# Reading the spare bank ahead of the maxima, and spreading the ungrouping copies, in four attention stages of a sixteen-stage kernel

## The reference

```python
scores = jnp.einsum('bhqd,bhkd->bhqk', q, k) / jnp.sqrt(jnp.float32(D_K))
scores = jnp.where(causal, scores, -jnp.inf)
attn = _my_softmax(scores, axis=-1)          # exp(x - max) / (sum + eps)
ctx = jnp.einsum('bhqk,bhkd->bhqd', attn, v)
...
return ctx @ Wo.T + bo
```

## Time and profile before

| | |
|---|---|
| median of 3 runs | 4516.43 us (4515.83 to 4519.06) |
| profiled execution | 4499.53 us, span 4497.8 us |
| granted TensorE clock, mean | 0.804 |
| TensorE busy | 3027.0 us, 67% |
| VectorE busy | 2776.0 us, 62% |
| GpSimd busy | 2034.3 us, 45% |
| ScalarE busy | 1710.5 us, 38% |
| ungrouping copies (L1007), 128 | 39.6 us in all, mean 310 ns |
| l0b, steps with exponentials | 582 to 1105 us |
| l2a | 2214 to 2568 us |
| l2b | 2856 to 3212 us |
| l3a | 3494 to 3848 us |

### The profile page before, as it was taken

How to read it: one execution, slowest core, us unless ns; L and a number is a source line. 1 busy time by engine, 2 the same in 40 slices (tenths; PEclk the granted TensorE clock), 3 DMA queues, 4 the chain that set the end, 5 groups by cost and what they waited for, 6 DMA issues and landing times. The chain is left out here.

```text
span 4497.8 us, 67760 instructions
## 1 busy us (share of the span) xinstructions
PE 3027.0 (67%) x23775; PEld 1875.0 (42%) x23775; DVE 2776.0 (62%) x5980; ACT 1710.5 (38%) x3042; POOL 2034.3 (45%) x2610
## 2 busy tenths in 40 slices
PE   5858277776286568659587756777566888466856
PEld 3658112121286248558233334333243344244534
DVE  4634477774534852342577578677487767495778
ACT  2413256665122223434355512455422455223511
POOL 6553320100243313232445376354595454595776
PEclk9879578887588669879699867799777999586967
DMA  5122222210122012002221000222001211000000
GB/s 157 39 71 76 66 82 66 63 53 1 49 90 61 9 44 70 19 25 63 73 79 66 23 1 1 86 72 73 2 0 44 72 66 52 1 1 1 1 1 19
DMA packets 217167, 206.35 MB, mean 46 GB/s; under 512 B 49431, under 2 KB 194007, under 8 KB 216072
## 3 DMA queue, kind: packets, MB, share of 16 engines
q1 hardware_dynamic: 204552, 176.85, 12.2%
q0 software_dynamic: 12288, 25.19, 1.8%
HBM read 103.55 MB, written 96.47 MB: 44 GB/s over the span
## 5 line engine op out<-in xcount | busy, mean ns | idle before, releaser
L942 DVE TENSOR_REDUCE l0b_negm<-l0b_ps_s 128x2 f32<-128x1024 f32 x256 | 304.2, 1220 | 139.0 <-PE l0b_ps_s L713 138.3
L802 ACT ACTIVATE l0b_E<-l0b_ps_t 128x1024 f32<-128x1024 f32 x256 | 262.0, 1023 | 198.3 <-PE l0b_ps_t L695 197.9
L942 DVE TENSOR_REDUCE l2b_negm<-l2b_ps_s 128x2 f32<-128x256 f32 (+3 forms) x256 | 199.2, 819 | 83.2 <-PE l2b_ps_s L719 82.9
L942 DVE TENSOR_REDUCE l3a_negm<-l3a_ps_s 128x2 f32<-128x256 f32 (+3 forms) x256 | 199.1, 818 | 79.7 <-PE l3a_ps_s L719 79.2
L942 DVE TENSOR_REDUCE l2a_negm<-l2a_ps_s 128x2 f32<-128x256 f32 (+3 forms) x256 | 198.6, 819 | 73.7 <-PE l2a_ps_s L719 73.4
L802 ACT ACTIVATE l3a_E<-l3a_ps_t 128x768 f32<-128x768 f32 (+1 forms) x192 | 169.2, 881 | 166.7 <-PE l3a_ps_t L695 166.4
L802 ACT ACTIVATE l2a_E<-l2a_ps_t 128x768 f32<-128x768 f32 (+1 forms) x192 | 169.4, 882 | 162.6 <-PE l2a_ps_t L695 162.4
L802 ACT ACTIVATE l2b_E<-l2b_ps_t 128x768 f32<-128x768 f32 (+1 forms) x192 | 169.4, 882 | 143.0 <-PE l2b_ps_t L695 142.9
L883 POOL TENSOR_SCALAR_AFFINE_SELECT l2b_E<-l2b_E 128x256 f32<-128x256 f32 x256 | 101.0, 408 | 214.0 <-ACT l2b_E L802 213.8
L883 POOL TENSOR_SCALAR_AFFINE_SELECT l3a_E<-l3a_E 128x256 f32<-128x256 f32 x256 | 101.0, 407 | 200.2 <-ACT l3a_E L802 198.2
L883 POOL TENSOR_SCALAR_AFFINE_SELECT l2a_E<-l2a_E 128x256 f32<-128x256 f32 x256 | 101.0, 407 | 198.3 <-ACT l2a_E L802 196.0
(11 more groups left out here) (1013 smaller groups left out, 9392.2 us busy)
## 6 DMA issues: line engine op xcount, KB each, us to landing
room_up<-l0b_stack SPq DMA_DIRECT2D x32, 192.0 KB
room_down<-l0b_stack SPq DMA_DIRECT2D x32, 192.0 KB
room_up<-l2a_stack SPq DMA_DIRECT2D x32, 192.0 KB
room_down<-l2a_stack SPq DMA_DIRECT2D x32, 192.0 KB
room_up<-l2b_stack SPq DMA_DIRECT2D x32, 192.0 KB
room_down<-l2b_stack SPq DMA_DIRECT2D x32, 192.0 KB
room_up<-l3a_stack SPq DMA_DIRECT2D x32, 192.0 KB
room_down<-l3a_stack SPq DMA_DIRECT2D x32, 192.0 KB
```

The lines of the kernel that those rows point to most:

```text
L802: act.activation(probs(n % 3, c, 0)[:, 2 * p:2 * p + 2, :], ps_t[:, :, 0:width[c]], ACT.Exp, scale=scale).then_inc(probs_ready.sem, 1)
L942: e = dve.tensor_reduce(negm[:, qt, :, j], ps_s[n % 2][:, :, off:off + keys[qt]], AX.X, ALU.max, negate=True)
```

## The change

In VectorE's loop, `weighted` (l = 4) and `add_output` (group 1, l = 2) move ahead of `maxima` in their step, in all four stages. In l0b alone the 16 ungrouping copies are laid one a step on the steps of `UNGROUP_AT`, 5 to 24 of the next batch, and `ao` gets a second tile, so that sums of the next batch don't overwrite what is still to be copied; the copies of the last batch for which no step is left follow the loop. The total of instructions is the same.

```diff
@@ -447,7 +447,7 @@
 K_ROWS = (slice(2, 5), slice(0, 6, 5), slice(1, 2))
 STACK = 48
 M_ROW = 48
-UNGROUP = (0, 3, 6, 7, 10, 13, 16)
+UNGROUP_AT = (5, 6, 8, 9, 10, 11, 13, 14, 15, 16, 17, 18, 19, 21, 22, 24)
 
 
 def heads_attention_stage(core, name, w, wo=None, bo=None, qk_bias=None, v_bias=None, rope=None, eps=0.0,
@@ -495,7 +495,7 @@
         oT = sb("oT", [P, S])
         den = sb("den", [P, TB, 4])
         rec = sb("rec", [P, TB, 4])
-        ao = sb("ao", [P, TB, D])
+        ao = [sb(f"ao{u}", [P, TB, D]) for u in range(2 if grouped else 1)]
         if projected:
             aoT = sb("aoT", [P, S])
         y = sb("y", [P, TB, D])
@@ -767,7 +767,7 @@
                         mm = pe.transpose(ps_x[:, t * P:(t + 1) * P], oT[:, t * P:(t + 1) * P], core.identf[:, :])
                 elif what == "attnT":
                     for t in range(TB):
-                        mm = pe.transpose(ps_x[:, t * P:(t + 1) * P], ao[:, t, :], core.identf[:, :])
+                        mm = pe.transpose(ps_x[:, t * P:(t + 1) * P], ao[0][:, t, :], core.identf[:, :])
                 else:
                     for t in range(TB):
                         mm = pe.matmul(ps_x[:, t * P:(t + 1) * P], aoT[:, t * P:(t + 1) * P], wo[:, :], start=True, stop=True)
@@ -991,21 +991,20 @@
                 c = G % QUADS * 32
                 if projected and c == 0 and G > 0:
                     in_spare(dve, "attnT", G // QUADS - 1)
-                dve.tensor_tensor(ao[:, :, c:c + 32].rearrange("p t (h d) -> p t h d", d=HD),
+                dve.tensor_tensor(ao[G // QUADS % len(ao)][:, :, c:c + 32].rearrange("p t (h d) -> p t h d", d=HD),
                                   pv[:, :, :, 0:HD], r, ALU.mult).then_inc(spare_read.sem, 1)
 
-            def ungroup(n, part):
-
-                if part == 0:
+            def ungroup(n, k):
+
+                i, j = k // 4, k % 4
+                if k == 0:
                     dve.wait_ge(spare_read.sem, spare_read.upto(use["back", QUADS * n + 3] + 1))
                     if n >= 1:
                         dve.wait_ge(out_read.sem, out_read.upto(n))
-                for k in range(UNGROUP[part], UNGROUP[part + 1]):
-                    i, j = k // 4, k % 4
-                    src = ao[:, :, :].rearrange("p k (t i d) -> p t k i d", t=4, i=4)[32 * j:32 * j + 32, :, :, i, :]
-                    dst = y[:, :, :].rearrange("p t (k j d) -> p t k j d", k=4, j=4)[32 * i:32 * i + 32, :, :, j, :]
-                    e = dve.tensor_copy(dst, src)
-                if part == len(UNGROUP) - 2:
+                src = ao[n % 2][:, :, :].rearrange("p k (t i d) -> p t k i d", t=4, i=4)[32 * j:32 * j + 32, :, :, i, :]
+                dst = y[:, :, :].rearrange("p t (k j d) -> p t k j d", k=4, j=4)[32 * i:32 * i + 32, :, :, j, :]
+                e = dve.tensor_copy(dst, src)
+                if k == len(UNGROUP_AT) - 1:
                     e.then_inc(out_ready.sem, 1)
 
             def add_output(n):
@@ -1039,10 +1038,12 @@
             rows.statistics(dve, ch, 1)
             rows.shifts(dve, 1)
             for T, b, g, l in steps():
+                if l == 4 and 0 <= QUADS * b + g - 1 < QUADS * B:
+                    weighted(QUADS * b + g - 1)
+                if g == 1 and l == 2 and projected and 0 <= b - 1 < B:
+                    add_output(b - 1)
                 if 0 <= T + 3 * L < ALL:
                     maxima(T + 3 * L)
-                if l == 4 and 0 <= QUADS * b + g - 1 < QUADS * B:
-                    weighted(QUADS * b + g - 1)
                 if g == 0 and 0 <= b + 2 < B:
                     if rope is not None and l in (0, 1, 2, 5):
                         rotate({0: "q", 1: "q_swapped", 2: "k", 5: "k_swapped"}[l], b + 2)
@@ -1055,12 +1056,10 @@
                     rows.shifts(dve, n)
                 for n in named(counted, T):
                     rows.statistics(dve, ch, n)
-                if grouped and 0 <= b - 1 < B and 0 <= g * L + l - 5 < len(UNGROUP) - 1:
-                    ungroup(b - 1, g * L + l - 5)
+                if grouped and 0 <= b - 1 < B and g * L + l in UNGROUP_AT:
+                    ungroup(b - 1, UNGROUP_AT.index(g * L + l))
                 if g == 0 and l == L - 1 and 0 <= b < B:
                     split_maxima(2 * b + 1)
-                if g == 1 and l == 2 and projected and 0 <= b - 1 < B:
-                    add_output(b - 1)
                 if g == 1 and l == 5 and v_bias is not None and 0 <= b + 1 < B:
                     n = b + 1
                     in_spare(dve, "v", n)
@@ -1073,6 +1072,10 @@
                     split_maxima(2 * (b + 1))
                 if g == 3 and l == 0 and out_normed and 0 <= b - 1 < B:
                     normalise(b - 1)
+            if grouped:
+                for k, at in enumerate(UNGROUP_AT):
+                    if at >= L + 3:
+                        ungroup(B - 1, k)
             if out_normed:
                 normalise(B - 1)
             dve_step.per = ch.k
```

## The result

The changed kernel takes 4395.8 us (median of 4 runs, 4391.5 to 4403.0); the kernel before took 4516.1 us beside it (4508.9 to 4519.1). The ratio of the runs is 0.9737, 95% interval 0.972 to 0.9755: 119 us or 2.6% less by the ratio, 120 us by the medians, against a forecast of 90 us and 4426.4 us. It lies inside the range of 4392 to 4472, 4 us from its lower end.

A forecast was written before the change was run, and what follows sets the result against it. No engine is full; a circle of waits paces the four stages, TensorE often waiting for VectorE. Causal stages 65.5 (73.5 less 8) plus l0b 24.5 make 90 us off: 4426.4 us, range 4392 to 4472.

The forecast's parts named there:

- signs of being right: `ao` and `y` waits under 5 us; l2a, l2b, l3a 19 to 25 shorter each, l0b 20 to 30; copy mean under 0.31.
- `v`: Causal stages, value projection (L757): its waits for `ao` all go once `back` is read in VectorE's idle time, 26.2 us.
- Output product: Causal stages, transposes of the maxima after the output product (L762): waits for `y` all go, 26.3 us.
- Swapped keys: l2a and l3a, swapped key projection (L753): of 13.2 us waiting for `ao`, 10 times 0.7 = 7 us.
- Maxima: Causal stages, score products' waits for `negm`: 14 of 30.4 us (6, 4 and 4), bounds 0 and 30.
- The 8 us taken off: Causal stages: TensorE, coming sooner, meets ScalarE still copying `oT`; about 0.3 us in 21 places, with odd ends 8 us.
- the term for the clock: l0b: shorter waits keep the clock nearer 2.4 GHz; 5 us at half clock in five batches, 3 us, bounds 0 and 12.
- The collisions: l0b steps 8 to 11: single copies meeting GpSimd; one collision, 1 us, bounds 0 and 4 x 1.2 us a batch.
- More comes back: Rival: causal `negm` waits but 5 go (11 us more), 10 more in l0b, 9 of clock: 120 us, 4396; chance 0.09.
- half of the 90: Rival: waits move on to VectorE's rotations, `oT` or the DMA of the maxima; only half gained, 4471; chance 0.13.
- the DMA of the maxima: Next thing late after the causal edits: placing the maxima; covered by 0.75 us, else each 0.1 us short costs 2 us.
- first reduction of a score pair: Rival, slower: it becomes the gate since reads precede it; 105 us added against 90 - 14 won, 4545; chance 0.03.

The follow-up runs named there:

- first fillers: Kernel before plus five needless products per l0b batch (from the second) in TensorE's wait at step 10, three ahead of the first score pair, two ahead of the second: 4499.0 us.
- copies spread: Kernel before with only the ungrouping copies laid one a step and the second tile for the sums; maxima stay first: 4471.4 us, ratio 0.9946.
- late copies: Changed kernel with the 16 ungrouping copies on steps 11 to 30, none on steps 5 to 10: 4365.6 us, ratio 0.9726.
- one copy: Changed kernel with one plain 128 x 512 copy per batch on step 24 in place of the 16 ungrouping copies: 4364.5 us, ratio 0.9719.
- reads first: Kernel before with only `weighted` and `add_output` moved ahead of the maxima in all four stages, ungrouping copies as before: 4394.6 us, ratio 0.9776.
- `weighted` only: Kernel before with only `weighted` (l = 4) moved ahead of the maxima; `add_output` stays behind them: 4424.8 us, ratio 0.9855.
- second profile: The changed kernel run once more, nothing altered: 4391.8 us, ratio 0.9728.
- fillers: Needless products in TensorE's step-10 wait: five on the kernel before, 4499.0 us; three on the reads-moved kernel, 4403.5; two on the changed kernel with needless VectorE reductions, 4400.0.
- the stop: Changed kernel with two needless VectorE reductions of 128 x 1024 ahead of `split_maxima` in batches 1 to 7 of l0b: 4397.6 us, ratio 0.9795.

## Why the prediction was right, and where its sizes were not

**The mechanism.** TensorE's waits for the spare bank were on the path: moving `weighted` and `add_output` alone gives 101 us of the 119 (first experiment), and leaving `add_output` out gives 30 of them back. Of the signs of being right, the waits for `ao` and `y` came out at 4.3 us (under 5 forecast), l0b's copies at a mean of 0.27 us and its waits for `negm` at 15.5 (about 17); the stages gained as forecast or more. The sizes were too small by a third, and the time is in the range with some luck: its lower end was made of a larger gain for `negm` and of at most 12 us for the clock, and the gain for `negm` was no larger.

**Causal stages, 65.5 forecast, 82.5 measured.** By terms, in l2a, l2b and l3a: `v` 26.2 forecast, the waits for `ao` are gone. Output product 26.3 forecast; 1.5 left. Swapped keys 7 forecast of 13.2: here I was too careful, since the wait for `ao` went whole and only 2.1 us for `k_turn` at L770 came in its place. Maxima 14 forecast; 30.4 fell to 17.9, so 12.5, of which l2b gave 2.9 of my 4. The 8 us taken off: the waits for `oT` grew by 3.7, 1.5 and 2.5 us, 7.7 in all, which was right; but in l2b 3.3 us of waits for `m_piece` and in all three 6.9 us for `mT` went too, which the sum did not have. It did not have the growth of others either: 7.9 us for ScalarE's exponentials and 3.0 for GpSimd's masking. With these, all of TensorE's waits in the three stages fell by 66.6 us, 1.1 us from the forecast, its misses having cancelled. The rest is TensorE's busy time, 16.6 us less, 13.6 of it in l3a, whose clock was 0.94 before and 0.98 after in the two profiles. Against the run with 0.98 and the old order (348.1 us) l3a gained 23.2 and the three stages 73.1.

**l0b, 24.5 forecast, 43.5 measured.** The step that failed is the term for the clock, "I take 3, bounds 0 and 12", together with how the waits were added. The waits for `negm` came out as forecast: 31.1 to 15.5 (17 forecast). But `ao` left 2.8 of 8.8, by the collision at step 11, and the waits for ScalarE's exponentials grew by 10.5 and those for `mT` by 3.9, so that TensorE's waits as a whole fell only from 127 to 121 us. What fell is its busy time, 388.3 to 351.5 us with the same instructions. In the third batch, from the transposed scores of step 8 to those of step 16, the kernel before takes 23.16 us and the changed one 17.50. Of these 5.66 us, all waits of TensorE together make 2.1 (8.07 to 6.00; those for `negm` alone 5.23 to 1.79); the remaining 3.6 are instructions that took half again to twice as long in the old one: 1.94 us in place of 1.06 for the value products, 1.86 for 1.16 in the projection. In 737 to 742 us the clock is 1.00 where the earlier trace rows have 0.50.

**What the lower clock cost.** The granted clock in these traces is 1.00 or 0.50 and nothing between, so its time at 0.50 can be added up for a stage. Stages of the same code in different profiles then give a price:

| stage, code (profiles) | length, us | at 0.50, us |
|---|---|---|
| l2a, old order (before, first fillers, copies spread) | 354.1, 356.6, 361.6 | 19.5, 28.7, 47.4 |
| l3a, old order (copies spread, before) | 348.1, 357.5 | 13.4, 44.1 |
| l2a, new order (late copies, one copy, changed) | 325.0, 327.0, 329.0 | 14.2, 20.5, 28.5 |
| l0b, reads first (`weighted` only, both) | 499.1, 506.1 | 116.8, 144.3 |
| l0b, changed (first profile, second) | 479.9, 479.9 | 87.3, 104.5 |

From the ends of the first three rows, a microsecond at the lower clock makes a causal stage 0.27 to 0.31 us longer. In l0b the two rows give 0.25 and 0, but the batches of equal programs, compared one by one (three pairs of profiles, 24 pairs of batches), give 0.27 by a line through zero. The changed kernel spends 87 us of l0b at 0.50 (105 in the second profile), where the kernel before spends 179; so, as an estimate, 20 to 25 of the 43.5 us go with the clock, and 19 to 24 are left for the waits, where the forecast had 21.5 without its clock term. The first two experiments agree: reads first, 34 us less at 0.50, so 9 of the 17.3 us, and 8 left for the 8.8 of `ao`; copies spread, 65 us less, so 18 of the 31.3, and 13.6 left for the 14 forecast. The term was mis-sized because it took one stretch of 5 us in five batches, 25 us; the kernel before has 84 us at 0.50 in steps 10 to 15 alone, of which 5 are left (24 in the second profile), and 69 in steps 16 to 23, of which 55 are left.

That is a rate between profiles, not an experiment on the clock. Where only the clock was treated, nothing was won: fillers left l0b at 523.3, 516.5 and 497.9 us against 523.4, 506.1 and 485.5. The first fillers did cut the time at 0.50 by 51 us, worth 14 at this rate, and the added products cost as much. What they also show is that slow TensorE and late VectorE lie side by side: with either left, the other's gain is met by a wait (1.59 us at 740.82). The changed kernel shortened VectorE's queue, and then both went. A treatment of the clock that adds no work was not found.

**The collisions, 1 us a batch forecast.** In the third batch three of the four single copies on steps 8 to 11 met GpSimd's split, against the one that I counted, and cost 1.7 us more than undisturbed copies (0.60 + 1.14 + 0.63 - 3 x 0.22); over the five batches with splits it is 1.2 us a batch. But my picture of the group was wrong as well: the 2.59 us in the earlier trace rows are three copies and not one, and all three were drawn out (line L1007 of the kernel before in 738 to 741 us: duration in ns, min/median/max, as in the earlier trace rows):

```profile
L1007 DVE COPY l0b_y<-l0b_ao x3: 661/678/1223, 738.1 to 739.4; 32x128 f32<-32x128 f32 x3
```

In the whole stage the kernel before has 22 copies over 0.3 us and the changed one 14, and the copies' time fell from 39.6 to 34.0 us: spreading them made fewer collisions, not more. Moving them behind the split left 5 and won 9.9 us in l0b. The Trainium skill (SBUF — State Buffer, Who interferes with whom) tells of such a meeting as a lock on a port pair, and the drawn-out copies agree. The reductions of l0b kept 1.21 to 1.23 us, beside the same GpSimd instructions too. The same section of the Trainium skill says that this reduction never contends on this chip; the trace agrees.

**The rivals.** The time is that of "More comes back" (120 us, 4396), which I gave 0.09, and so is l0b's sum: 24.5 + 10 + 9 = 43.5. That is luck on its side too, for its terms are only half right: `negm` gave nothing beyond my own forecast, 17.9 us of it and not 5 stayed in the causal stages, and what came instead were `mT`, the swapped keys and TensorE's faster instructions. The others fell: `oT` took 7.7 us and not half of the 90, the DMA of the maxima appears in no list, and no first reduction of a score pair became a gate.

## What to carry to other kernels

When an engine has a read that frees a bank and a reduction whose input the same producer issues later, put the read first: it fits into the idle time, and the length of the producer's wait in the timeline is nearly what it is worth. Small copies of VectorE belong where it idles and where GpSimd is quiet, not just apart from each other; leaving them out altogether (a run with one plain copy) says in one number whether a place is free. Compare stage by stage over several profiles, and look at the time at the lower clock beside the length: two stages of equal code differed by up to 9 us with it, and a gain below that is told apart only between profiles with the same share of slow time.

## What I had not expected of the hardware

- Time outside the edited stages came in two levels, 2902 to 2908 and 2918 to 2926 us, as it seems by set of runs.
- The same stage with the same program varied with TensorE's granted clock: l2a 354.1 us at 0.97 and 361.6 at 0.93, l3a 357.5 at 0.94 and 348.1 at 0.98, l0b 506.1 and 499.1 at 0.86 and 0.88.
- Time at the lower clock costs less than the half that TensorE's own instructions lose: 0.27 to 0.31 us of causal stage length for each microsecond, by stages of equal code.
- After a wait of 2.5 to 3 us at step 10 of the third batch the clock stood at 0.50 for the next step or more in the kernel before, with the reads first and with the stop; after 0.41 and 1.38 us in the changed one it stayed at 1.00. But the second profile of that same program has a batch in which it fell after 1.39 us (below), so the wait at step 10 alone does not decide it. Keeping the clock up there with needless products moved slow stretches to later steps.

```profile
853.01 0.39 PE L713 MATMUL l0b_ps_s<-room_down,room_up 48*128 48x512 bf16 x2 [1.39 <-DVE l0b_negm L942]
854.39 0.61 PE L713 MATMUL l0b_ps_s<-room_down,room_up 48*128 48x512 bf16 x2 [0.99 <-DVE l0b_negm L942]
```
